# Unread products taken out of the first three steps of the last stage

## What is computed

```
x = x + tanh(g_xattn[0]) * linear_attention(layernorm(x), ctx, ctx)
x = x + tanh(g_ffn[0])   * ffn_4bit(layernorm(x), ...)
x = x + tanh(g_xattn[1]) * autocorrelation(layernorm(x), ctx, ctx)
x = x + tanh(g_ffn[1])   * ffn_dora(layernorm(x), W, ...)

def autocorrelation(q, k, v):            # per head
    corr = ifft(fft(q) * conj(fft(k))).real
    w, idx = top_k(corr, 11);  w = softmax(w)
    out = sum_i w_i * v[min(idx_i + pos, L - 1)]
```

## Time and profile before

| | us |
|---|---|
| median of 3 runs | 2080.0 (2079.57 to 2080.14) |
| the profiled execution | 2078.76 |
| its span | 2077.0 |
| TensorE busy in the span | 2007.4 (97%) |
| VectorE busy | 1103.7 (53%) |
| ScalarE busy | 1192.7 (57%) |
| GpSimd busy | 695.1 (33%) |

### The profile page before, as it was taken

One profiled execution on the slowest core, in us unless ns is written; L12 is line 12 of the kernel. 1 busy time (PEld: TensorE's weight loads), 2 busy tenths in 40 slices (PEclk: granted clock), 3 DMA queues, 4 the chain that ended last, 5 costly groups with the idle time before them and its releaser, 6 DMA issues. The chain is left out here.

```text
span 2077.0 us, 25938 instructions
## 1 busy us (share of the span) xinstructions
PE 2007.4 (97%) x9596; PEld 1007.7 (49%) x9596; DVE 1103.7 (53%) x1956; ACT 1192.7 (57%) x1871; POOL 695.1 (33%) x649
## 2 busy tenths in 40 slices
PE   6996999999999999999999999999998899999998
PEld 5773444444444444444444444444444455555544
DVE  5776252342724426244262532524358988888872
ACT  6995656756666565665657666565644434443431
POOL 3343211112112121221212122121147776677742
PEclk9998999999999999999999999999999999999999
DMA  6642212323112212122221211111122101111001
GB/s 222 198 154 72 72 51 67 92 62 87 49 49 66 76 51 78 47 77 82 61 62 55 73 57 51 51 53 45 51 71 91 36 36 51 51 46 41 26 21 41
DMA packets 66349, 141.48 MB, mean 68 GB/s; under 512 B 9136, under 2 KB 13872, under 8 KB 66224
## 3 DMA queue, kind: packets, MB, share of 16 engines
q1 hardware_dynamic: 66224, 139.83, 21.0%
HBM read 127.21 MB, written 12.58 MB: 67 GB/s over the span
## 5 line engine op out<-in xcount | busy, mean ns | idle before, releaser
L785 ACT ACTIVATE first<-first 128x512 f32<-128x512 int32 x1008 | 632.7, 628 | 28.0
L1269 PE MATMUL a_psQ<-xT_hi,gu 128*128 128x512 f16 x1376 | 417.7, 380 | 1.8 <-DVE rel L1051 1.8
L1269 PE MATMUL a_psC<-xT_hi,gu 128*128 128x512 f16 x1376 | 416.4, 379 | 0.0
L1040 DVE SCALAR_TENSOR_TENSOR wt<-first,w_scale,absm 128x512 f32<-128x512 f32 x132 | 99.6, 755 | 473.7 <-ACT first L785 472.3
L920 POOL TENSOR_TENSOR gu<-wt,gu 128x512 f16<-128x512 f32 x88 | 104.4, 1186 | 721.5 <-ACT gu L791 721.5
L1269 PE MATMUL a_psQ<-xT_lo,gu 128*128 128x512 f16 x688 | 261.3, 380 | 0.0
L1269 PE MATMUL a_psC<-xT_lo,gu 128*128 128x512 f16 x688 | 260.7, 379 | 0.0
L1269 PEld LDWEIGHTS a_psQ<-xT_hi,gu 128*128 128x128 f16 x1376 | 135.0, 98 | 163.1 <-DVE rel L1051 2.3
L1269 PEld LDWEIGHTS a_psC<-xT_hi,gu 128*128 128x128 f16 x1376 | 134.4, 98 | 160.0
L1821 PE MATMUL a_psL<-xT_lo,l_x 128*128 128x512 f16 x768 | 170.5, 379 | 2.5 <-DVE l_x L1914 2.5
L920 POOL TENSOR_TENSOR dn_lo<-wt,dn_hi 128x512 f16<-128x512 f32 x42 | 48.6, 1157 | 337.2 <-ACT dn_hi L791 337.2
(11 more groups left out here) (350 smaller groups left out, 3474.8 us busy)
## 6 DMA issues: line engine op xcount, KB each, us to landing
first<-in_codes SPq DMA_DIRECT2D x132, 256.0 KB, 3.0
absm<-in_absmax SPq DMA_DIRECT2D x264, 128.0 KB, 3.2
X<-in_x SPq DMA_DIRECT2D x16, 512.0 KB, 4.3
c_in<-in_ctx SPq DMA_DIRECT2D x16, 512.0 KB, 5.3
cT<-in_ctxT SPq DMA_DIRECT2D x16, 512.0 KB, 3.5
o_sp<-in_w SPq DMA_DIRECT2D x16, 512.0 KB, 3.7
xT_hi<-in_ctx SPq DMA_DIRECT2D x8, 1024.0 KB, 7.0
out<-X SPq DMA_DIRECT2D x15, 512.0 KB, 2.6
```

Source lines behind the costliest of these rows:

```text
L785: act.activation(level[u % 2][:], codes[u % RING] if k == 0 else level[u % 2][:], ACT.Prelu, bias=bias, scale=scale, alpha=alpha).then_inc ...
L1040: dve.scalar_tensor_tensor(wt[u % 2][:], source[:], w_scale[:, m:m + 1], absm[u % RING][:], ALU.mult, ALU.mult).then_inc(scaled, 1)
L1269: mm = pe.matmul(o[:], w[c][:, m, k, :], xx[:, k, ts], start=(q == 0), stop=(q == 3 * KD - 1))
```

## The change

It takes out `keep_on`, its four calls and the four waits ahead of them. Nothing is put in their place, and all the other instructions keep their order.

```diff
-                def keep_on(out, count):
-
-                    for _ in range(count):
-                        pe.matmul(out, fwd_hi[:, 0, :], fwd_hi[:].rearrange("p k j -> p (k j)"), start=True, stop=True)
-
...
                 for n in range(2):
                     weight_turn(n)
-                    pe.wait_ge(k_done, n + 2)
-                    keep_on(psE[:, 0, :], 6)
                     weight_even(n)
...
                     if now is not None:
                         linear(now, 0)
-                    if n == 2:
-                        pe.wait_ge(k_done, n + 2)
-                        keep_on(psE[:, 0, :], 5)
                     if n < N:
                         weight_even(n)
                     if n == 2:
                         corr(n + 1, range(CH // 2))
                         weight_odd(n)
                         corr(n + 1, range(CH // 2, CH))
-                        pe.wait_ge(prod_done, 2 * n + 4)
-                        keep_on(psQ[:, 0, :], 7)
```

## The result

| | before | after |
|---|---|---|
| median of 17 runs | 2080.21 us (2079.43 to 2085.14) | 2084.24 us (2079.81 to 2084.84) |
| ratio | | 1.0014, 95% interval 1.0008 to 1.0021 |
| the profiled execution | 2078.76 us | 2084.28 us |
| its span | 2077.0 us | 2082.5 us |
| from the stage's first products to the even spectrum of step 3 | 81.97 us | 86.57 us |

The kernel became slower: by the ratio 2.9 us (1.7 to 4.4), by the medians 4.0 us. The two measures differ; both kernels scatter over 5 us, and not in the same shape: 11 of the 17 runs after lie between 2084.19 and 2084.84, the other six between 2079.81 and 2083.45, while before 14 of 17 lie under 2081.4. By the bound of 0.2% the ratio is within no change, the median almost on it.

A forecast was written before the change was run, and what follows sets the result against it. In steps 0 to 2 the path alternates between TensorE and VectorE; behind them TensorE bounds the kernel. Direct 0.0 plus clock 1.5 x 0.95 = 1.4 us on 2080.0 gave 2081.4 us, range 2079.4 to 2083.8.

The forecast's parts named there:

- Direct term: Steps 0 to 2 of the last stage: the removed products, 5.0 us of TensorE, lie inside waits that stay; 0.0 us.
- The clock as the place of the cost: Longer TensorE rests of 2.37 to 2.70 us in steps 0 to 2 lose some clock: 1.4 us, 2081.4, chance 0.40.
- nothing happens: Rival: no fall of the clock at any place, rests shorter than the harmless 2.67 us; 2080.0 us, chance 0.36.
- One or two of the five places: Four longer rests in steps 0 to 2 and the stage's entry: 1.5 falls counted, at 0.95 us each.
- The price of one fall: 1.85 us lost at half clock less idle time behind: 1.1, 0.5, 1.05 and 1.15 us, mean 0.95.
- The fifth place: Stage entry at half clock: a later rise meets the opened rest of step 0; about 1.1 us, up to twice that.
- Transposes don't count: Rival: transposes don't keep the clock up, so rests at all three turns cost a fall; 2.65 us, 2082.65, chance 0.08.
- the range: Forecast bounds for the median after the change: 2079.4 to 2083.8 us.
- the sum of all four falls: Falls in all four longer rests of steps 0 to 2: 1.1 + 0.5 + 1.05 + 1.15 = 3.8 us, 2083.8.
- The class: Whole kernel against no change, bound 0.2% or 4.2 us: within 0.83, slower by more 0.14, faster by more 0.03.
- The fourth rival: Half clock from the entry stays 6.7 us in step 0, falls in the other three rests; 5.3 us, 2085.3, chance 0.12.
- point of decision: Half level covering 8.3 us of TensorE's unbroken work in the three steps, half of it 4.16 us, 0.2%.

The follow-up runs named there:

- the narrow products: Kernel before with its 24 unread products and their waits kept, each product only 16 columns wide: 2084.78 us against 2080.56 (ratio 1.0014).
- the four single runs: Kernel before (2080.3 us) with one group of unread products out: step 0 2083.23 us, step 1 2080.43, step 2 first 2082.64, step 2 last 2082.48.
- the transposes: Kernel before with every unread product replaced by two 128x128 32-bit transposes of the unit matrix: 2080.28 us against 2080.56 (1.0000).

## Why the prediction was right, and where it was off

- *Direct term 0.0.* Right. The even spectra begin where VectorE's low part lets them, with rests of 2.37 to 2.38 us as worked out, and the narrow products show it from the other side: with the instructions and waits kept, the time of before doesn't come back.
- *The clock as the place of the cost.* Right, by the four single runs, each with its own half level in its profile, and by the narrow products and the transposes. The rival "nothing happens" (0.36) took the shortness of the rests, 2.37 us against 2.67 in the first stage, for protection. It is none: behind the same 2.67 us the clock fell in 4 of 14 profiles. The sentence beside it, that the work on either side of a rest is broken too, was the one that counted, and it got too little weight.
- *How many fall: the step that failed.* "One or two of the five places" were four in the profile after. Of the 17 runs 11 lie at 2084.2 to 2084.8 with it, at a mean clock of 0.989 to 0.991; which falls each of them had isn't seen.
- *The price of one fall.* 0.95 us was the mean; the profile after has 4.60 / 4 = 1.15. The way it was worked out, work at half level less the idle time behind, holds for the odd spectra: they come 0.80, 0.18 and 0.73 us later in steps 0 to 2, where 1.1, 0.5 and 1.05 were foretold; the half level lay on some 3.4 us of work, not 3.7. It doesn't hold for what follows. By place: step 0 1.1 foretold and 1.7 measured, of which 1.0 is the long `nmax` on VectorE, a term that the sum didn't have; step 1 0.5 and 0.0 (0.7 when alone, where the fall came in the rest); step 2 1.05 + 1.15 = 2.2 and 2.7, since the first fall put VectorE back, so that the rest ahead of the key's odd spectrum grew to 3.21 us (+0.5), and since the idle time of 0.69 us behind the second fall was not used up but moved along (0.66 us after), so that this fall cost 1.4.
- *The fifth place*, a late rise at the entry: the way to the first even spectrum grew by 0.2 us in the profile after, and by 0.3 us in profiles that still had the group of step 0. It is scatter that both kernels share, not a cost of the change.
- *Transposes don't count* (0.08): refuted.
- *The size.* +1.4 us foretold; +2.9 (1.7 to 4.4) by the ratio, +4.0 by the medians. The median of 2084.24 lies 0.4 us above the range, whose upper end was the sum of all four falls, 3.8 us; set against the ratio, 2080.0 x 1.0014 = 2082.9, it lies inside. The class, within 0.2%, is right by the ratio and near its edge by the median.
- *The fourth rival* (2085.3) had the nearest time, but not the mechanism: the half level didn't stay from the entry, it came back four times. Its point of decision, 8.3 us of unbroken work under the half level, was passed (four stretches of about 3.5 us), and part of it was still hidden: 14 us at half level would be 7 us lost, 4.6 were, and of these 1.0 was the long `nmax`.

## What to carry to other kernels

An unread product may be doing a job: before it is taken out, look at what TensorE's rest becomes and at the granted clock around it, and count the work on both sides of the rest, not the rest alone. A rest at full clock in one profile is no proof: the same rest of step 15 was followed by a fall in 5 of 10 profiles, and that of the first stage in 4 of 14. So compare the times of many runs, and more than one profile, before a fall is put down to a place. Fill such a rest with wanted work where there is some, or with transposes; and price a fall at each place by following its delay into the other engines, since four half levels of the same length cost 0 us in one step and 1.7 us in the step before, and over half of the latter came from one VectorE instruction that now met a GpSimd operation.

## What the hardware showed that was not expected

- Rests of 2.37 to 3.21 us were followed by 1.2 GHz in all four places of the profile after and in all four single ones. With the narrow products (2.23 to 2.55 us behind them) it was one of four, the rest of 2.53 us in step 15 was followed by it in 5 of 10 profiles, and that of 2.67 us in the first stage in 4 of 14. In the second stage rests of 1.88 and 0.48 us, 0.6 us of products between them, were enough.
- The fall comes late: in the four places after the change the clock was still at full when the work began again, and the half level of some 3.4 us covered nothing but work. With one group out it also came within the rest, 0.4 us before its end in step 1 and over 0.7 us before it in step 2, where it lasted 6.8 us.
- The small VectorE instruction that writes `nmax` took 0.17 us in one alignment and up to 1.18 us where it began early in a GpSimd operation, with whose end it ended. Here that turned a delay of 0.8 us into 1.7.
- The scatter of this kernel, 5 us over 17 runs, is in good part the clock's. In the profiles whose instructions are the same up to there, the last stage begins at 1581.49 to 1584.28 us. The parts that change length without a change of the program are the first stage (1.5 us where the clock falls behind the rest of 2.67 us), the start of the second stage (half level until 189.4 to 193 us) and the rest in step 15 (1.65 us).
